# Gate and up products of a four-layer residual kernel by Strassen's scheme: seven block products for eight

## What is computed

```python
def lora_add(base, inp, A, B):                       # A, B picked per batch, rank 16
    t = jnp.einsum('bri,bni->bnr', Ab, inp)
    return base + jnp.einsum('bor,bnr->bno', Bb, t) * SCALE
gate = lora_add(jnp.einsum('bnh,fh->bnf', x, W_gate), x, A_gate, B_gate)
up = lora_add(jnp.einsum('bnh,fh->bnf', x, W_up), x, A_up, B_up)
act = jax.nn.silu(gate) * up
down = lora_add(jnp.einsum('bnf,hf->bnh', act, W_down), act, A_down, B_down)
return x + down
```

## Time and profile before

| | us |
|---|---|
| median of three runs | 314.36 (313.09 to 315.21) |
| the profiled execution | 314.33 |
| its span in the profile | 312.5 |
| gate/up chunks 1 to 10, on PE | 121.25 to 240.45 |
| PE busy, DVE busy, ACT busy | 303.2, 147.8, 103.7 |

### The profile page before, as it was taken

One profiled execution on the slowest core, in us unless ns is written; L12 is line 12 of the kernel. 1 busy time (PEld: TensorE's weight loads), 2 busy tenths in 40 slices (PEclk: granted clock), 3 DMA queues, 4 the chain that ended last, 5 costly groups with the idle time before them and its releaser, 6 DMA issues.

```text
span 312.5 us, 4638 instructions
## 1 busy us (share of the span) xinstructions
PE 303.2 (97%) x1690; PEld 249.8 (80%) x1690; DVE 147.8 (47%) x246; ACT 103.7 (33%) x162; POOL 25.1 (8%) x39
## 2 busy tenths in 40 slices
PE   6889899999999999999999999999999999999995
PEld 5358688988888788888888888888888888888884
DVE  0298997895569536143143142232623934233003
ACT  1375662513336245033133133133531742221000
POOL 2084500620100000000000000000000000000000
PEclk9999999999999999999999999999999999999999
DMA  5979982005306510421422412470430000022004
GB/s 178 339 271 350 394 279 78 0 0 158 113 0 171 160 35 0 134 90 48 134 76 58 133 69 66 130 281 0 146 81 0 2 2 0 0 69 67 0 2 134
DMA packets 23888, 33.21 MB, mean 106 GB/s; under 512 B 3264, under 2 KB 16064, under 8 KB 23744
## 3 DMA queue, kind: packets, MB, share of 16 engines
q1 hardware_dynamic: 23584, 32.48, 32.0%
q10 hardware_dynamic: 288, 0.52, 0.5%
HBM read 30.89 MB, written 2.10 MB: 106 GB/s over the span
## 4 chain that ended last, share of the span: by engine, by line
PE 90%; SPq 4%; DMA 3%; DVE 2%; issue 0%; ACT 0%
PE bank L964 25%; PE bank L965 25%; PE bank L966 24%; PE bank L1073 3%; DMA w_raw<-in_w 3%; SPq L310 3%; PE bank L918 2%; PE bank L937 2%; PE bank L1120 2%; PE bank L1011 1%; PE bank L898 1%; PE bank L948 1%; PE bank L950 1%; PE bank L949 1%; SPq L330 1%; PE bank L1049 1%
## 5 line engine op out<-in xcount | busy, mean ns | idle before, releaser
L964 PE MATMUL bank<-xb,wgu_hl 128*128 128x512 f32 x176 | 69.3, 394 | 0.0
L965 PE MATMUL bank<-xb,wgu_hl 128*128 128x512 f32 x176 | 69.0, 392 | 0.0
L966 PE MATMUL bank<-xb,wgu_hl 128*128 128x512 f32 x176 | 68.5, 389 | 0.0
L826 DVE TENSOR_TENSOR act_f<-bank,act_f 128x512 f32 (+1 forms) x22 | 15.2, 691 | 79.4 <-PE bank L1073 75.0
L966 PEld LDWEIGHTS bank<-xb,wgu_hl 128*128 128x128 f32 x176 | 33.1, 188 | 7.2
L964 PEld LDWEIGHTS bank<-xb,wgu_hl 128*128 128x128 f32 x176 | 33.0, 188 | 5.9 <-issue 0.2
L965 PEld LDWEIGHTS bank<-xb,wgu_hl 128*128 128x128 f32 x176 | 33.2, 189 | 5.2
L964 PE MATMUL bank<-act_hl,wd_hl 128*128 128x512 f32 (+1 forms) x99 | 36.5, 369 | 0.0
L965 PE MATMUL bank<-act_hl,wd_hl 128*128 128x512 f32 (+1 forms) x99 | 36.3, 367 | 0.0
L966 PE MATMUL bank<-act_hl,wd_hl 128*128 128x512 f32 (+1 forms) x99 | 36.2, 366 | 0.0
L561 ACT ACTIVATE act_f<-bank 128x512 f32 (+1 forms) x22 | 13.2, 598 | 64.6 <-PE bank L1073 64.6
(11 more groups left out here) (126 smaller groups left out, 427.7 us busy)
## 6 DMA issues: line engine op xcount, KB each, us to landing
w_raw<-in_w SPq DMA_DIRECT2D x22, 256.0 KB, 7.4
wgu_raw<-in_wgu SPq DMA_DIRECT2D x11, 512.0 KB, 3.4
bgu_raw<-in_bgu SPq DMA_DIRECT2D x88, 64.0 KB, 2.2
w_raw<-in_w SPq DMA_DIRECT2D x7, 512.0 KB, 7.5
wd_raw<-in_wd SPq DMA_DIRECT2D x4, 704.0 KB, 5.2
out<-x_f SPq DMA_DIRECT2D x7, 256.0 KB, 2.4
x_f<-in_xT SPq DMA_DIRECT2D x6, 256.0 KB, 7.3
w_raw<-in_w SPq DMA_DIRECT2D x1, 1024.0 KB, 5.0
```

The lines of the kernel that those rows point to most:

```text
L826: dve.tensor_tensor(dst, bank[5 + 2 * h][:], dst, ALU.mult).then_inc(act_mul, 1)
L964: pe.matmul(dst, w_hi, x[0][:, cols], start=start, stop=False)
L965: pe.matmul(dst, w_hi, x[1][:, cols], start=False, stop=False)
L966: return pe.matmul(dst, w_lo, x[0][:, cols], start=False, stop=stop)
```

## The change

Chunk 0 is computed as before. Chunks 1 to 10 form five pairs (f1, f2). For each pair and for gate and up separately (a step n, ten in all: gate n even, up n odd) the product [A11 A12; A21 A22] x [B11 B12; B21 B22] is made, A's rows being the two chunks, A's columns the halves of D, B's columns the halves of the tokens. Winograd's form of Strassen's scheme is used: S1 = A21+A22, S2 = S1-A11, S3 = A11-A21, S4 = A12-S2; T1 = B12-B11, T2 = B22-T1, T3 = B22-B12, T4 = B21-T2. DVE forms the S before the split (`form_s`, 4 x 256 elements a step) and the T once (`form_t`, 4 x 1024 elements); T are split too (`xt_high`, `xt_low`). Seven block products, each of 2 x 3 matmuls of 512 columns, replace eight. Because partial sums enter several outputs, ACT copies four partial results a step from PSUM to SBUF (`copy_part`) and DVE adds four (`add_c`); silu and the product then read SBUF. A step uses banks 0 to 3 (gate) or 4 to 7 (up); up's weights lie in one buffer, gate's in another. The products of a pair come once both its steps are done.

`bgu_raw` still has two slots, one for each chunk of a pair; their 16 loads are issued together, after `bgu_ready` of the pair's up step. The down weights are loaded after the last weight split and are split chunk by chunk behind the last step (`wd_high`, `wd_low`), one 512-element piece ahead of each `act_high` and `act_low`. The selection matrix `t3_sel` and others move to other addresses, and GpSimd prepares them after layer 1.

Loads, on SP:

```diff
-            with sp.Fori(0, 4) as i:
...
+            sp.wait_ge(bgu_ready, 1)
+            load_bgu(2)
+            sp.wait_ge(main_done, 16)
+            load_bgu(1)
+            load_wgu(3)
+            load_wgu(4)
+            for p in range(1, PAIRS):
+                sp.wait_ge(bgu_ready, bgu_count(2 * p - 1, 1))
+                load_bgu(2 * p + 1)
+                load_bgu(2 * p + 2)
+                if p + 1 < PAIRS:
+                    sp.wait_ge(wc_lo, 3 * 2 * p)
+                    load_wgu(2 * p + 3)
+                    load_wgu(2 * p + 4)
```

ACT, start of layer 3 and the steps:

```diff
             t3_copy(0)
+            for k in range(2):
+                xt_high(k)
             t3_high(0)
             t3_copy(1)
+            xt_high(2)
+            odd_silu(0)
             t3_high(1)
+            odd_silu(1)
+            for i in range(2):
+                bgu_high(0, i)
+            xt_high(3)
+            for n in range(2 * PAIRS):
+                p, g = divmod(n, 2)
+                more = n + 1 < 2 * PAIRS
+                if g == 1:
+                    for k in (2, 3):
+                        silu(p, k)
+                if more:
+                    wc_high(n + 1, 0)
+                copy_part(n, 0)
+                if more:
+                    wc_high(n + 1, 1)
+                copy_part(n, 1)
+                if more:
+                    wc_high(n + 1, 2)
+                copy_part(n, 2)
+                if more:
+                    for i in range(2):
+                        bgu_high(n + 1, i)
+                if g == 0:
+                    for k in (0, 1):
+                        silu(p, k)
+                copy_part(n, 3)
```

DVE, behind `t2_low(1)`, then the start of layer 3 and the steps:

```diff
-            gate_up_lo(1, 1, 2)
-            residual(2, 1, [])
+            for k in (0, 2, 1, 3):
+                form_s(0, k)
+            for part_of in range(3):
+                wc_low(0, part_of)
+            x_add(2, 1, 0)
+            x_add(2, 1, 1)
+            x_low(2, 1, 0)
+            form_t(0)
+            x_low(2, 1, 1)
+            x_add(2, 1, 2)
+            x_low(2, 1, 2)
+            x_add(2, 1, 3)
+            form_t(1)
+            x_low(2, 1, 3)
+            for k in range(2, 4):
+                form_t(k)
+            for k in range(2):
+                xt_low(k)
...
             t3_low(0)
+            xt_low(2)
+            odd_product(0)
             t3_low(1)
+            odd_product(1)
+            for i in range(2):
+                bgu_low(0, i)
+            xt_low(3)
+            for n in range(2 * PAIRS):
+                p, g = divmod(n, 2)
+                more = n + 1 < 2 * PAIRS
+                if more:
+                    form_s(n + 1, 0)
+                    form_s(n + 1, 2)
+                if n > 0:
+                    for k in (2, 3):
+                        add_c(n - 1, k)
+                if more:
+                    form_s(n + 1, 1)
+                    wc_low(n + 1, 0)
+                    form_s(n + 1, 3)
+                if n > 0 and g == 0:
+                    for k in (2, 3):
+                        act_product(p - 1, k)
+                add_c(n, 0)
+                if more:
+                    for part_of in (1, 2):
+                        wc_low(n + 1, part_of)
+                if g == 1:
+                    act_product(p, 0)
+                add_c(n, 1)
+                if more:
+                    for i in range(2):
+                        bgu_low(n + 1, i)
+                if g == 1:
+                    act_product(p, 1)
```

PE, a step; `product` is 2 x 3 matmuls of 512 columns, `lora3` two of 256:

```diff
+            def step3(n):
+                p, g = divmod(n, 2)
+                f1, f2 = chunks_of(n)
+                x, w, y, z = (bank[4 * g + k] for k in range(4))
+                pe.wait_ge(wc_lo, 3 * n + 1)
+                if n >= 2:
+                    pe.wait_ge(c_added, 4 * (n - 1))
+                product(x, n, A11, x_block(0, 0), True, True).then_inc(p1_done, 1)
+                product(w, n, A12, x_block(1, 0), True, False)
+                pe.wait_ge(bgu_ready, bgu_count(n, 0))
+                lora3(w, f1, g, 0).then_inc(c11_ready, 1)
+                pe.wait_ge(wc_lo, 3 * n + 2)
+                product(y, n, S1, t_block(0), True, True).then_inc(p5_done, 1)
+                pe.wait_ge(part_copied, 4 * n + 1)
+                product(x, n, S2, t_block(1), False, True).then_inc(p6_done, 1)
+                pe.wait_ge(part_copied, 4 * n + 2)
+                product(y, n, S4, x_block(1, 1), False, False)
+                lora3(y, f1, g, 1).then_inc(c12_ready, 1)
+                pe.wait_ge(part_copied, 4 * n + 3)
+                product(x, n, S3, t_block(2), False, True).then_inc(p7_done, 1)
+                pe.wait_ge(wc_lo, 3 * n + 3)
+                product(z, n, A22, x_block(0, 1), True, False)
+                pe.wait_ge(bgu_ready, bgu_count(n, 1))
+                lora3(z, f2, g, 0).then_inc(c21_ready, 1)
+                pe.wait_ge(part_copied, 4 * n + 4)
+                lora3(x, f2, g, 1).then_inc(c22_ready, 1)
```

More of the change, by code:

```diff
@@ L57 @@
 ACT_RING = 8
+PAIRS = FC // 2
+A11, A12, A22, S1, S2, S3, S4 = range(7)
 def bass_four_residual_layers(nc, xT, ids0, ids1, ids2, ids3, w0, w1, aw1, b1, w2, a2, b2, bias2,
@@ L141, in bass_four_residual_layers @@
         ident = own("ident", [P])
[L142 to L146, removed]
+        sel_raw = at("sel_raw", o_tp, [4 * P + 1])
         sel_r = own("sel_r", [3, P], F32R)
@@ L567, in act_high, with wd_high @@
                 high(act_hl[i % ACT_RING][:, 0], act_f[:, f, cols]).then_inc(act_hi, 1)
[L569 to L572, removed]
+            def wd_high(f):
+                if f == 0:
+                    for o in range(C):
+                        act.wait_ge(wd_in[o], 16)
+                high(wd_hl[:, f, 0], wd_raw[:, :, f]).then_inc(wd_hi, 1)
             def td_copy(h):
@@ L614, in _ @@
-            for i in range(ACT_RING, PIECES):
+                if i == 7:
+                    for h in range(H):
+                        td_high(h)
+            act.wait_ge(bd_in, 16 * B)
+            high(bd_st[:], bd_raw[:]).then_inc(bd_hi, 1)
+            for i in range(FC, PIECES):
                 act_high(i)
@@ L886, in _ @@
+            dve.wait_ge(bd_hi, 1)
+            low_rows(bd_st[:], bd_raw[:]).then_inc(bd_ready, 1)
+            for i in range(FC, PIECES - C):
                 act_low(i)
@@ new lines, in lora3, with odd_lora, x_block, t_block @@
+                return ins
+            def odd_lora(g, h):
+                lora3(bank[4 + 2 * h + g], 0, g, h, shared=False).then_inc(up_done if g else gate_done, 1)
+            def x_block(d, h):
+                cols = slice(h * HT, (h + 1) * HT)
+                return [[xb[:, i, 2 * d + c, cols] for c in range(2)] for i in range(2)]
+            def t_block(k):
+                return [[xt[k][:, i, c] for c in range(2)] for i in range(2)]
+            def product(dst, n, a, x, start, stop):
+                w = wc[1 - n % 2]
+                for c in range(2):
+                    hi, lo = w[:, 0, a, c], w[:, 1, a, c]
+                    pe.matmul(dst[:], hi, x[0][c], start=(start and c == 0), stop=False, skip_group_check=True)
+                    pe.matmul(dst[:], hi, x[1][c], start=False, stop=False, skip_group_check=True)
+                    ins = pe.matmul(dst[:], lo, x[0][c], start=False, stop=(stop and c == 1), skip_group_check=True)
+                return ins
```

380 lines of the change are left out of this document (248 added, 132 removed).

## The result

| | us |
|---|---|
| median of four runs after | 317.64 (315.93 to 318.79) |
| median of four runs before, on the same chip | 314.76 (313.09 to 315.21) |
| ratio, after to before | 1.0105, interval 1.0074 to 1.0136 |
| the profiled execution after, its span | 315.93, 314.2 |

The forecast was 315.6 (range 309.5 to 322.5). The time is slower by about 1%: the median lies 2.0 us above the forecast, inside the range, but 0.1 us past the 317.5 from which the forecast counted "slower by over 1%" (chance 0.36). The profiled execution, for which the sum was made, lies 0.3 us above the forecast.

The account below looks back on a forecast made before the run. PE's matmuls were taken to bound the kernel. From 314.33 us: -13.7 for dropped matmuls, +3.35 and +1.7 at layer 3's start, +9.3 for low-rank loads, +0.6 for restarts gave 315.6 us, range 309.5 to 322.5.

Parts of the forecast that it names:

- slower by over 1%: Outcome class for the whole kernel: a measured time over 317.5 us, chance 0.36.
- What goes: PE in the ten steps: 42 matmuls for 48, 10.55 us a step if nothing waits, -13.7 us in all.
- One step: Within a step, ACT's copy of S1's product releases PE at 5.31, needed at 5.72: slack 0.4 us.
- the same within 0.1: Gate steps: ACT's 1024 elements ahead of the S1 copy end as in up steps, within 0.1 us.
- DVE holds each step up: Rival: four `form_s` behind two `add_c` delay the S1 copy, 0.6 us a step, 321.6 us; chance 0.30.
- The low-rank loads: Up steps: the next pair's 16 loads land late; PE loses 2.3 us in each of four pairs, +9.3.
- The start of layer 3: PE waits for DVE's `t3_low(0)`, +3.35 us, and in step 0 for the S1 copy, +1.7.
- The rest: Down weights and GpSimd's copies behind layer 1 cost 0; restarting PE after six stalls costs +0.6 us.
- Restarts: PE's first matmul after each of six stalls takes 0.49 us for 0.39, +0.6 in all.
- shows anything but 9: Sign against the forecast: the profile's clock row has a value other than 9.
- take over 11 us: Sign against the forecast: gate steps on PE last more than 11 us.
- The clock falls: Rival: behind longer PE waits one step runs at 1.2 GHz, +10.5 us, 326 us; chance 0.04.

Follow-up runs that it names:

- version with both edits: Changed kernel with its 16 low-rank loads per pair joined into 8 issues and layer 3's start reordered (`t3_low(0)` first, early ACT copies in step 0): 302.08 us, ratio 0.9623.
- One added instruction: One unused 256-element DVE subtraction ahead of each step's last `form_s`, added to the changed kernel with joined low-rank loads and reordered layer 3 start: 303.83 us, ratio 0.9733.
- the run with three added subtractions: Three dependent 256-element DVE subtractions ahead of each step's last `form_s`, added to the changed kernel with joined low-rank loads and reordered layer 3 start: 308.78 us, ratio 0.9835.
- the repeated run: The changed kernel run again unaltered beside the last experiments: 317.65 us, ratio 1.0107; its profiled execution took 318.31 us.

## Why the forecast was right

- **"What goes": right.** 10.55 a step; steps without a wait or a low clock took 10.53 to 10.65, and a chunk with 42 matmuls and nothing else changed 10.56. 60 instructions fewer.
- **"One step": right.** The S1 copy let PE go before it was needed in every step behind step 0, at 81% DVE; the slack is 0.46 in up steps of the version with both edits, for 0.4 forecast. One added instruction doesn't end it in any step behind step 1, three do. In gate steps it is 1.3, not "the same within 0.1": that half was wrong and cost nothing. The rival *DVE holds each step up* is refuted by runs; its chance of 0.30 was too high, since the spacing in the earlier trace rows holds beside a dense ACT too.
- **"The low-rank loads": right in place and chain, 0.4 too high.** The forecast counts PE's loss from where PE would have gone on, and the profile's waits leave out 0.16 of that (shown in the run with three added subtractions). Four waits listed as 2.56, 2.27, 1.72 and 1.71 are 8.9 us by starts, for 9.3. They are unequal: the first two sets of sixteen issues took 11.10 and 10.72 us, the others 10.25 and 10.23, and step 2 was stretched by the clock. In the last two pairs each link was a little shorter than forecast: the loads landed 12.0 after DVE's end for 12.26 (spacing 0.652 for 0.656, landing 2.1 for 2.2), and from the landing to PE it was 1.17 for 1.31. Joining the issues two by two took all four waits away.
- **"The start of layer 3": right.** Step 0 began 3.2 later behind the layer's start for 3.35; the S1 copy released PE at t = 7.38 of step 0 for 7.4, 1.6 late for 1.7. What that was worth as a cure was less than it cost, 3.2 of 4.6 us, as long as the load waits stood behind it.
- **"The rest": down at nothing, right** (72.1 us from the last step to the end, 72.0 before). Restarts: 0.10 to 0.15 for each of the five stalls in the steps, about as the earlier trace rows had it.
- **The clock: a term that was missing.** The forecast had it at 2.4 GHz throughout, and as signs against itself that the row "shows anything but 9" and that gate steps "take over 11 us"; the row has a 7, and step 2 takes 12.11. The rival *The clock falls* had the mechanism and an overdrawn price: 1.5 us for a stretch, not a whole step of 10.5. The Trainium skill ("TensorE: Matmul & The Clock Gate", section "Why this matters for your kernels"), whose warning about idle gaps stood beside that rival, had the direction right; the rows of before, with no wait over 1.42 us behind the first matmul, could not show it. The waits of this kernel are shorter than the gaps that the page speaks of, so its rule, read with them, did not make this rival the forecast, though the prediction says so. The trace decides: the clock fell behind them too.

The sum by measured terms, from 314.33: -13.7 + 3.2 (start) + 1.6 (step 0) + 8.9 (loads) + 0.8 (restarts and small rests) + 1.5 (clock) - 0.7 (layer 3 began at 104.46 for 105.20: less waiting in layer 0, ahead of all that was changed here) + 0.1 (behind the last step) = 316.0, for 315.93 measured. That the forecast came within 0.3 us of the profiled execution is in part luck: the 1.5 of the clock, which it lacked, stood against 0.65 too much in waits and the 0.7 from layer 0. The median of all runs is 1.7 us above the profiled one, whose granted clock (0.993) was the highest of the four. In the profile of the repeated run a second low stretch (1.6) and layer 0 (0.9) make such a difference; for these four runs it was not recorded.

## What to carry to other kernels

Fewer instructions on the bounding engine are worth their full price only if every hand-off of the new order is on time; list what is queued behind each waiting instruction (here a PSUM copy behind a load) and count the issues of a small-DMA load as work on its queue. Before giving up such a change, look for the wait's cause in the issue count and in the order of a stage's first few instructions: two small edits turned +1% into -4%. Look at the waits together, since part of the gain of one (here 0.8 of 3.8 us) can be eaten by the next. To price a stall, measure between starts: the listed wait is shorter than the time lost.

## What was not expected of the hardware

- The clock fell behind some waits and not behind others of like length. In layer 3 it did at 2.56, 2.58, 3.37 and, in two profiles, the start's 2.65 and 2.66, and in the run with three added subtractions 1.2 us behind a wait of 1.87; it did not at the start's 2.67 in another profile, nor at 2.27, 2.14, 1.72 and 1.71. In layer 0 it fell once behind 1.14, 1.43 and 0.37 in a row. The low stretches lasted 3.2 to 3.5 us and cost about 1.5 where their cost can be read. What decides is open.
- A stall costs PE about 0.28 us beyond the wait that the profile lists: 0.17 by which the record of a matmul (0.39) outlasts its spacing (0.23), and 0.10 at the first matmul behind the wait.
- A DMA issue with twice the bytes cost SP 0.80 in place of 0.65 us, and landed in 2.6 for 2.1 us: joining two saves 0.5 of 1.3 us on the queue. The issues of one kind are not all alike: sixteen took 10.23 to 11.63 us in these traces.
